# Attention layer 0: where the weighted values and projected keys are put in PSUM, and the order of TensorE, VectorE and ScalarE in a block

## The reference, cut to what matters

```
x = x + attention0(layernorm(x), ctx)      # 32 query heads of 128, 8 key/value heads
x = x + ffn0(layernorm(x))                 # fp8-like grid, 1792 inner
x = x + attention1(layernorm(x), ctx)
x = x + ffn1(layernorm(x))

attention0: q = x @ wq; k = ctx @ wk; v = ctx @ wv     # q: 32 heads, k, v: 8
            p = softmax(q k^T / sqrt(128))             # per sequence of 64
            out = concat(p v) @ wo
```

## Time and profile before

| | us |
|---|---|
| median of 3 runs | 1713.1 (1711.9 to 1725.19) |
| profiled execution | 1715.58 |
| its span | 1713.9 |
| busy PE / DVE / ACT / POOL | 1489.9 / 1325.1 / 876.0 / 477.8 |

### The profile page before, as it was taken

The page is one execution under the profiler, slowest core; times in us unless marked ns, Lnnn a source line. Parts: engine busy times, 40 slices in busy tenths (PEclk is TensorE's granted clock), DMA queues, the critical chain, the costliest instruction groups (busy, mean ns, idle before and its releaser), DMA issues. The chain is left out here.

```text
span 1713.9 us, 33213 instructions
## 1 busy us (share of the span) xinstructions
PE 1489.9 (87%) x12523; PEld 923.0 (54%) x12523; DVE 1325.1 (77%) x2414; ACT 876.0 (51%) x1825; POOL 477.8 (28%) x397
## 2 busy tenths in 40 slices
PE   5689989899899899899899986779999998677686
PEld 4456566566566666666566663334445454344343
DVE  6567767777678678668578688689999985999777
ACT  4334425335335334334335333488989863888652
POOL 4513303204214114124123101001111103689620
PEclk8799999999999999999999998989999999999898
DMA  8343435345345353453543431222222260766402
GB/s 319 141 118 119 122 106 138 104 118 136 94 121 132 94 161 93 106 172 68 143 135 84 132 142 25 100 44 44 44 56 51 43 126 1 133 103 113 86 1 98
DMA packets 283642, 178.54 MB, mean 104 GB/s; under 512 B 240240, under 2 KB 256752, under 8 KB 278768
## 3 DMA queue, kind: packets, MB, share of 16 engines
q1 hardware_dynamic: 244608, 143.49, 34.0%
q10 hardware_dynamic: 38896, 33.03, 6.2%
HBM read 102.04 MB, written 18.87 MB: 71 GB/s over the span
## 5 line engine op out<-in xcount | busy, mean ns | idle before, releaser
L806 PE MATMUL xp<-WO,OT 128*128 128x512 f16 x1536 | 345.0, 385 | 6.9 <-DVE X L1060 6.9
L700 POOL TENSOR_TENSOR QT<-QA,QT 128x512 f16<-128x512 f32 x96 | 113.5, 1196 | 646.3 <-ACT QT L884 646.3
L806 PEld LDWEIGHTS xp<-WO,OT 128*128 128x128 f16 x1536 | 149.2, 99 | 194.3 <-issue 18.7
L749 PE MATMUL xp<-XR,WQ 128*128 128x256 f16 x1536 | 185.1, 274 | 3.9 <-DVE QA L990 3.9
L909 ACT ACTIVATE E<-E 128x512 f32<-128x512 f32 x64 | 40.3, 629 | 268.2 <-DVE E L1037 268.2
L1288 PE MATMUL db<-W0T,XD 128*128 128x448 f16 x768 | 152.1, 359 | 23.1 <-DVE XD L1487 23.1
L749 PEld LDWEIGHTS xp<-XR,WQ 128*128 128x128 f16 x1536 | 148.2, 98 | 28.0 <-issue 6.1
L749 PE MATMUL pj<-XR,WQ 128*128 128x256 f16 x1152 | 143.6, 281 | 16.0 <-PEq L421 9.7
L1060 DVE SCALAR_TENSOR_TENSOR X<-xp,X 128x512 f32<-128x512 f32 x128 | 88.1, 689 | 86.2 <-PE xp L806 86.2
L1303 PE MATMUL eb<-W1T,DT 128*128 128x512 f16 x672 | 149.3, 382 | 4.2 <-ACT eb L1382 2.7
L884 ACT ACTIVATE QT<-QA 128x512 f16<-128x512 f32 x96 | 59.7, 630 | 156.0 <-DVE QA L990 156.0
(11 more groups left out here) (254 smaller groups left out, 2889.3 us busy)
## 6 DMA issues: line engine op xcount, KB each, us to landing
XR<-xsets SPq DMA_DIRECT2D x31, 1280.0 KB, 5.6
XR<-xsets SPq DMA_DIRECT2D x31, 512.0 KB, 4.5
W0T<-in_L_xattn_wq ACTq DMA_DIRECT2D x7, 1024.0 KB, 5.2
W0T<-in_L_xattn_wo ACTq DMA_DIRECT2D x7, 1024.0 KB, 6.8
CS<-in_ctx SPq DMA_DIRECT2D x4, 1024.0 KB, 10.1
X<-in_x SPq DMA_DIRECT2D x4, 1024.0 KB, 11.2
out<-X SPq DMA_DIRECT2D x8, 512.0 KB, 3.6
xsets<-XB SPq DMA_DIRECT2D x2, 1792.0 KB, 5.6
```

The lines of the kernel that those rows point to most:

```text
L700: pool.tensor_tensor(queries(1, i, j), query_sum(buffer), queries(0, i, j), ALU.subtract).then_inc(S["q_lo"], 1)
L749: last = pe.matmul(head_columns(Q_BANKS[n], m), WQ[:, a, Q_WEIGHTS[n], c, m * P:(m + 1) * P], XR[:, n, b, c, :].rearrange("p (b t) -> p b ...
L806: last = pe.matmul(xp[i % 2][:, :], OT[:, a, j, i * P:(i + 1) * P], WO[:, b, j, :], start=n == 0, stop=n == 3 * REP - 1)
```

## The change

- PE: keys go to bank tv0, values to pj1 (they wait for `add_query` 0); the second weighting goes to sc0, sc1 and follows the first directly; query products 5 and 6 come behind both. The first weighting also waits for `low_keys` of the next block (it reads tv0).
- DVE: softmax goes ahead of `add_query` 0 and `low_query`; then `add_query` 0, 1, `low_query`, `add_query` 2, `low_keys`, in t=0 the low WO, the pieces for FFN 0, `low_weights`, `low_values`, `low_out` 0, `add_query` 3, `low_out` 1, `add_query` 4. `low_q_sums` moves from POOL to DVE (t=2, after `accumulate` 1), `low_kv` to after `accumulate` 2.
- ACT: `high_keys` ahead of `high_query` 1; both `high_out` ahead of `high_query` 2, 3. `load_weights` moves from ACT's queue to SP's, behind the transposes of PT in t=0.
- Last group, t=2: `project_out` of tiles 0, 1, then the scores of the last block, then tiles 2, 3; DVE takes `accumulate` 0, 1 ahead of the last softmax.
- Opening: in blocks 1 and 2 the moments come right after the context tiles and the scales after set 3; in the last block the weights are split between the sets.

```diff
-        def low_q_sums(pool, g):
+        def low_q_sums(dve, g):
...
-                        if n == PER - 2 and blk < BLOCKS - 1:
+                        if n == (BT + 1 if blk else PER - 2) and blk < BLOCKS - 1:
                             ln_stats_scalar(act, 0, (blk + 1,))
+                        if blk == 3 and n == BT - 1:
+                            high_q(act, 0)
+                            high_kv(act, 0)
...
-                        if n == BT + 3 and blk < BLOCKS - 1:
+                        if n == (BT - 1 if blk else BT + 3) and blk < BLOCKS - 1:
                             dve.wait_ge(x_ld[blk + 1], 16)
                             ln_moments(dve, 0, blk + 1)
-                    if blk < BLOCKS - 1:
-                        ln_scales(dve, 0, blk + 1)
-                low_q(dve, 0)
-                low_kv(dve, 0)
+                        if n == (BT + 2 if blk else PER - 1) and blk < BLOCKS - 1:
+                            ln_scales(dve, 0, blk + 1)
+                        if blk == 3 and n == BT + 2:
+                            low_q(dve, 0)
+                        if blk == 3 and n == BT + 3:
+                            low_q_sums(dve, 0)
+                        if blk == 3 and n == BT + 4:
+                            low_kv(dve, 0)
...
+        weighed = (tv, sc)
...
+                    if t == 0 and g < GROUPS - 1:
+                        load_weights(sp, g)
...
             def project_keys(g, t):
-                pe.wait_ge(S["q_add"], n_of(g, t, 5, 1))
-                    last = pe.matmul(pj[1][:, :], WKV[:, a, k, 0, :], CT[:, b, k, tokens], start=n == 0, stop=n == 3 * KC - 1)
+                    last = pe.matmul(tv[0][:, :], WKV[:, a, k, 0, :], CT[:, b, k, tokens], start=n == 0, stop=n == 3 * KC - 1)
             def project_values(g, t):
-                pe.wait_ge(S["q11_lo"], n_of(g, t, 1, 1))
+                pe.wait_ge(S["q_add"], n_of(g, t, 5, 1))
...
-            def weigh_values(g, t, pair):
+            def weigh_values(g, t, pair, keys):
                 if pair == 0:
-                    pe.wait_ge(S["kv_lo"], n_of(g, t, 2, 2))
+                    pe.wait_ge(S["kv_lo"], n_of(*keys, 2, 1) if keys else n_of(g, t, 2, 2))
                     pe.wait_ge(S["pt_done"], n_of(g, t, 32, 32))
-                else:
-                    pe.wait_ge(S["ot_lo"], n_of(g, t, 4, 2))
...
-                    weigh_values(g, t, 0)
...
+                        project_values(*nxt)
+                    weigh_values(g, t, 0, nxt if more else None)
+                    weigh_values(g, t, 1, None)
                     if more:
-                        if early:
-                            project_values(*nxt)
-                        else:
-                            query_products(*nxt, (5, 6))
-                    weigh_values(g, t, 1)
-                    if early:
-                        scores(g, SPG - 1)
-                    project_out(g, t, more)
+                        query_products(*nxt, (5, 6))
+                    if last and t == SPG - 2:
+                        project_out(g, t, more, (0, 1))
+                        pe.wait_ge(S["ot_lo"], n_of(g, t, 4, 4))
+                        scores(g, SPG - 1)
+                        project_out(g, t, more, (2, 3))
+                    else:
+                        project_out(g, t, more, range(BT))
...
             def last_block(g, t):
+                accumulate(g, t - 1, 0)
+                accumulate(g, t - 1, 1)
                 scores_less_max(g, t, 0)
...
-                    if more:
-                        add_query(*nxt, 0)
                     for jp in range(2):
                         sums(g, t, jp)
                         normalise(g, t, jp)
                     low_probs(g, t, 0)
-                    if more:
-                        low_query(*nxt)
                     low_probs(g, t, 1)
                     if more:
+                        add_query(*nxt, 0)
                         add_query(*nxt, 1)
+                        low_query(*nxt)
+                        add_query(*nxt, 2)
+                        low_keys(*nxt)
...
                     low_out(g, t, 0)
                     if more:
-                            add_query(*nxt, 3)
-                            add_query(*nxt, 4)
+                        add_query(*nxt, 3)
                     low_out(g, t, 1)
+                    if more:
+                        add_query(*nxt, 4)
...
                         if i == 1 and t == SPG - 2 and not last:
+                            low_q_sums(dve, g + 1)
+                        if i == 2 and t == SPG - 2 and not last:
                             low_kv(dve, g + 1)
```

More of the change, by code:

```diff
@@ L495, in _ @@
                         sum_q(pool, 0)
-                low_q_sums(pool, 0)
             @block.tensor
@@ L647, in head_columns, with load_weights @@
             return bank[:, :].rearrange("p (b m t) -> p m b t", m=2, b=4)[:, m, :, :]
+        def load_weights(queue, g):
+            queue.wait_ge(S["xset_st3"], 16)
+            for t in range(2):
+                queue.dma_start(WB[:, 0:8, :].rearrange("p (c t) k -> p c t k", t=2)[:, :, t, :],
+                                w0[bass.ds(g * 256 + t * P, P), :].rearrange("p (c k) -> p c k", k=P)).then_inc(S["wb_ld"], 16)
+            for c in range(2):
+                queue.dma_start(WB[:, 8 + 4 * c:12 + 4 * c, :],
+                                w1[:, bass.ds(g * 256 + c * P, P)].rearrange("(t p) k -> p t k", p=P)).then_inc(S["wb2_ld"], 16)
         @block.sync
@@ L710, in group @@
                         sum_q(pool, g + 1)
-                    if t == SPG - 2:
-                        low_q_sums(pool, g + 1)
                     for n, lo, hi in prepared(t, last):
@@ L764, in project_values @@
                         own = slice(t * BLOCK + i * P, t * BLOCK + (i + 1) * P)
-                        last = pe.matmul(pj[0][:, i * P:(i + 1) * P], CT[:, a, k, own], WKV[:, b, k, 1, :],
+                        last = pe.matmul(pj[1][:, i * P:(i + 1) * P], CT[:, a, k, own], WKV[:, b, k, 1, :],
                                          start=n == 0, stop=n == 3 * KC - 1)
@@ L792, in weigh_values, with project_out @@
                             rows = slice(h * SEQ, (h + 1) * SEQ)
-                            last = pe.matmul(tv[h][:, s * 256:(s + 1) * 256], V[rows, t % 2, a, 2 * pair + s, :],
+                            last = pe.matmul(weighed[pair][h][:, s * 256:(s + 1) * 256], V[rows, t % 2, a, 2 * pair + s, :],
                                              PT[rows, b, :, 2 * pair + s, :], start=n == 0, stop=n == 2)
                 last.then_inc(S["pv_done"], 1)
-            def project_out(g, t, more):
+            def project_out(g, t, more, tiles):
                 pe.wait_ge(S["o_lo"], g + 1)
-                for i in range(BT):
+                for i in tiles:
                     pe.wait_ge(S["ot_lo"], n_of(g, t, 4, 2 * (i // 2) + 2))
@@ L815, in group @@
                         scores(g, t)
-                    early = last and t == SPG - 2
                     if more:
@@ L896, in high_out @@
                 for h in range(2):
-                    act.activation(o_out(0, pair, h), o_bank(h), ACT.Copy).then_inc(S["ot_hi"], 1)
+                    act.activation(o_out(0, pair, h), o_bank(pair, h), ACT.Copy).then_inc(S["ot_hi"], 1)
             def group(g, last):
@@ L918, in group @@
                                 high_weights(g, *p)
-                    early = last and t == SPG - 2
                     if more:
+                        high_keys(*nxt)
                         high_query(*nxt, 1)
@@ L925, in group @@
                         stats_x(act, t - 1)
-                    if t == 0 and not last:
-                        load_weights(act, g)
                     if more:
-                        high_keys(*nxt)
-                        if early:
-                            high_query(*nxt, 2)
-                            high_query(*nxt, 3)
-                        else:
-                            high_values(*nxt)
+                        high_values(*nxt)
                     high_out(g, t, 0)
+                    high_out(g, t, 1)
                     if more:
-                        if early:
-                            high_values(*nxt)
-                        else:
-                            high_query(*nxt, 2)
-                            high_query(*nxt, 3)
-                    high_out(g, t, 1)
+                        high_query(*nxt, 2)
+                        high_query(*nxt, 3)
                     if t == 1 and not last:
@@ L970, in _ @@
             high_query(0, 0, 0)
+            high_keys(0, 0)
             high_query(0, 0, 1)
-            high_keys(0, 0)
             high_values(0, 0)
@@ L1123, in group @@
                         first_x[1](dve)
-                    if more:
-                        add_query(*nxt, 2)
                     x_ahead(1)
@@ L1129, in group @@
                     if more:
```

(9 more changed lines are left out.)

30 lines of the change are left out of this document (7 added, 23 removed).

## The result

| | median, us | range | ratio to before, 95% |
|---|---|---|---|
| before | 1714.5 | 1711.9 to 1725.2 | |
| after | 1671.2 | 1669.7 to 1672.3 | 0.9735 (0.9693 to 0.9778) |

The profiled execution took 1672.3, with a span of 1670.4 at clock 0.956. I split both traces at the starts of the scores.

A forecast was written before the change was run, and what follows sets the result against it. TensorE was taken as the bound, busy 836 of 900 us. Gains of 5 (opening), 21, 2, -1, 6 (t=0 to 3) and 9 (last group) sum to 42: 1713.1 - 42 = 1671, range 1656 to 1697.

The forecast's parts named there:

- The mechanism of t=0: Loop, t=0: second weighting no longer late by 2.22, output projection 4.2 behind the first; gain 3.0 x 7 = 21.
- W: Start of a block's first weighting; in t=0 forecast at 604.6, the end of the values, against 605.24.
- e_lo: End of DVE's low_probs 1 in the softmax; forecast 0.95 sooner in t=0, with PT 4.1 behind it.
- t=1: 4.8 for 2: Loop, t=1: add_query 3, behind low_out 0 on DVE, becomes the projection's new wait; gain 0.3 x 7 = 2.
- t=2: 1.7 for -1: Loop, t=2: as t=1, but high_weights ahead of high probs 1 on ACT; projection at 669.2 against 669.07, loss 1.
- t=3: 11.0 for 6: Loop, t=3: wait for QA stays in part, first weighting at 694.3 against 695.17; gain 0.8 to 0.9, 6 over 7 blocks.
- P: Start of a block's output projection; without waits forecast 4.2 behind the start of the first weighting.
- Last group: 7.7 for 9: Last group's four blocks: 6.8 from the chain after t=2, with 1.9 of t=1 on top; 9 for the group.
- Opening: 2.6 for 5.3: Opening: sooner moments and scales, low_kv without its stall, first query products near 66.4; gain 5.3, bounds 2 and 6.
- C: Rival, chance 0.05: low_keys holds the first weighting in all 31 blocks with a next one; at 2 us, 1733.
- B: Rival, chance 0.15: add_query 3 decides the projection's start in t=0 and 3 too; loop gives 20 less, 1698.
- D: Rival, chance 0.13: low WO in t=0 and low_weights in t=3 collide with POOL's low query; 10 less gain, 1681.

The follow-up runs named there:

- loads_alone: The kernel before with only load_weights moved from ACT's queue to SP's, behind the transposes of PT in t=0; 1701.1, ratio 0.9901.
- loads_on_act: The changed kernel with load_weights back on ACT, behind high_keys and ahead of high_values; 1674.7, ratio 0.9738.
- softmax_undone: The changed kernel with add_query 0 back ahead of the sums and low_query between the two low_probs on DVE; 1659.5, ratio 0.9660.
- sums_on_pool: The changed kernel with low_q_sums back on POOL in the loop's t=2, the opening as changed; 1676.9, ratio 0.9751.
- rec_late: The changed kernel with weights_times_rec of t=2 moved on ACT behind both high_out; 1662.9, ratio 0.9697.

## Why the prediction was right, point by point

**The mechanism of t=0 held, and its size was 17.3 for 21.** The projection starts 4.05 behind the first weighting, with 4.2 forecast, and between the two the seven blocks gained 18.4 us, more than the 2.34 a block that was forecast. loads_alone shows that ACT's issue was the cause, loads_on_act that new banks and order are a second cure for it. What fell short is W. It was to come 0.64 sooner a block, with no wait for PT, and comes 3.3 us later in the sum of the seven, 7.8 us short. About half of that is more idle time inside the scores (2.9) and slower matmuls behind it (1.2), which vary from run to run. The other half is "PT arrived 4.1 after e_lo": it is 5.0 to 5.6, and PE still waits 4.5 us for PT in the seven blocks, where I had nothing. A PT later than 4.1 was named as a sign that the forecast is wrong; it cost 0.3 to 0.9 a block, inside the bound of 1 us. (The 0.3 to spare on add_query 3 is 0.5 by the prediction's own times; nothing hangs on it.) It is not the loads' place: 4.9 to 5.8 in the blocks that wait for PT with them on ACT, 4.9 to 5.5 behind XR; with softmax_undone it is 4.0 to 4.3. So all that the softmax order brought e_lo forward in t=0 was lost on the way to PT: in blocks whose first matmuls ran at full clock, e_lo is at 11.4 behind the scores instead of 12.7 to 13.0, and W at 17.0 instead of 16.8 to 17.1.

The DMA view shows where it is lost. The same six microseconds around the transposes of PT, in a t=0 of the change (454 to 460 us, e_lo at 454.12; each digit is the busy share of 0.15 us in tenths) and in a t=3 (542.3 to 548.3, e_lo at 542.44):

```profile
DMA  0000799999600999990000000000009999763348
q8 instruction: 1, 0.02, 1.8%
PT<-EH SPq DMA_TRANSPOSE x2, 3.8
```
```profile
DMA  0000599999800499999900000000059994509965
PT<-EH SPq DMA_TRANSPOSE x2, 2.8
```

The two transposes take a median of 3.8 us from issue to landing instead of 2.8. In t=0 a transfer of another queue (q8: one packet of 0.02 MB), named "instruction", falls into them. It starts 1.7 to 2.5 behind e_lo in all seven t=0 of the change, during the second transpose, and 0.7 to 1.0 behind it in before; the transposes' packets beside it take up to 2.1 us in the change, up to 1.2 in before, and 0.02 in any t=3, where no such transfer falls beside them. It comes at about the same place in the block while e_lo moves, so an earlier e_lo meets it in another transpose. No run moved it by itself: that it is the cause is likely and not shown.

**The softmax ahead of the query sums was mis-sized most.** I took e_lo 0.95 sooner in t=0 and 1, 0.55 in t=2 and 3. Against softmax_undone, which differs in this alone, e_lo is 0.0 sooner in t=2, 0.1 later in t=3, 1.2 to 1.5 sooner in t=0, where PT takes as much longer, and 1.16 in t=1, where nothing uses it. I had subtracted an operation's 0.68 from a chain in which DVE already waited for ACT. The two traces above show it to cost 7.0 us in the blocks of t=2; the medians differ by 12. In t=0 the median difference says little, as the clock there varies (below).

**t=1: 4.8 for 2.** add_query 3 ends at 610.53, 0.1 before the projection could start; I had put it 0.05 later than PE's own time. The forecast wait did not come, and the second weighting, 0.65 behind the first, gave the rest.

**t=2: 1.7 for -1, by luck.** Typical blocks went from 28.85 to 29.25, a loss of 0.4 where 0.1 was forecast, with the wait of 0.84 for add_query 3 that I had named. The sum is positive since one block of before took 33.4. There POOL's low_q_sums met another of DVE's pieces:

```profile
301.51 4.56 DVE L105 TENSOR_SCALAR VW<-VW 128x1024 uint32<-128x1024 uint32 x1
```

The accumulation behind L105 came late, the projection waited 2.41 for it, and the t=3 behind that block took 29.0 in place of 30.3 to 31.6.

**t=3: 11.0 for 6, of which 6.3 came where it was forecast, but by another path.** Summed over the seven blocks P stands 6.3 us nearer to the scores, as forecast. But I had 0.3 a block from the move of low_q_sums and 0.55 from the softmax order; it was 0.99 and nothing. L107 alone takes 0.68, not the 1.1 that I worked out from L1119. So the stall was 3.28 of its 3.96, and 1.0 of it remains when the 2.28 of low_q_sums are taken off: DVE's first reduce comes that much sooner, and e_lo with it. The right 6 is luck in its parts. Of the rest 4.1 is not the change's work on this block: idle time at the loop's turn that lay ahead of the turn's first score in before (4.4) and lies behind it now (0.3), where t=0 has it (14.1 before, 16.9 after). The wait for QA at the start is gone, not partly kept, and the new wait of 0.6 for low_kv did not come: no row of after has either. sums_on_pool and rec_late bring a wait for low_kv back (1.1 and 0.5), so it was near. In exchange the values wait 1.03 for add_query 0, which now stands behind the softmax on DVE: the later query sum has a second reader, project_values, that I had not priced. It cost nearly nothing only because PT lands at the time when the values end (W 14.76 behind the scores, 14.66 in softmax_undone).

**Last group: 7.7 for 9.** t=3 gave 6.6 for 6.8, t=1 2.2 for 1.9, t=0 0.4 for 0.3. In t=2, where I had booked nothing, P waited 4.82 and the block lost 1.4.

**Opening: 2.6 for 5.3.** The weights' part came as forecast: low_kv fell by 3.0 and low_q_sums moved without a stall. The sets' part did not: XN of block 3 started at 49.03 as said (49.1), but the splits behind it ran slower than the 11.2 a block, and scales that took 1.3 took 2.5 where they met POOL (L172 0.54 for 0.16, L174 1.13 for 0.17). The set that ACT's weight splits hold up came free at 58.1 and not 56.1, DVE's last split ended at 68.0 and not 65.8, and PE followed 1.1 later, not 0.6. The low bound of 2 was the better value.

The total of 43 (45.2 up to the end of attention 0) for 42 is thus right through errors that cancel: too much for t=0 and the opening (6.4), too little for t=1, 2 and 3 (10.5), 1.3 too much for the last group. Of the rivals, C did not occur (no weighting waits for KT), B's full wait neither; D's collision did in t=0 (3.27 for 2.28), and it was hidden. The Trainium skill, "SBUF — State Buffer", section "Who interferes with whom", says that a VectorE instruction with two SBUF inputs contends with a GpSimd one that reads SBUF. The low WO and L1038 are of that kind, and these rows agree: 3.27 for 2.28, and 1.44 for 0.69.

## What to carry to other kernels

Before moving an operation out of a chain, look whether the engine waits for another one inside that chain: if so, the operation was free there and will be late where it goes. Undo each part of a combined change by itself: of these four parts one cost time (7 us in t=2, 12 by the medians), and two removed the same wait. A queue has slots with slack and slots without: a load behind one that waits for a buffer inherits its wait.

## What the hardware showed that I had not expected

**The clock behind the loop's turn differs from turn to turn.** No run here shows what decides it. The same idle time, 2.56 and 2.54, comes before two t=0 blocks of the change; the first 24 query matmuls behind it then take 4.45 or 2.78:

```profile
326.68 1.24 PE L780 MATMUL sc<-KT,QT 128*128 128x64 f16 x37 [2.56 <-issue]
327.76 4.45 PE L754 MATMUL pj<-XR,WQ 128*128 128x256 f16 x24
...
445.76 1.24 PE L780 MATMUL sc<-KT,QT 128*128 128x64 f16 x37 [2.54 <-issue]
446.83 2.78 PE L754 MATMUL pj<-XR,WQ 128*128 128x256 f16 x24
```

The granted clock of the five microseconds behind (the eighth number) is 0.66 and 1.00, a part at the 1.2 GHz level and all at 2.4:

```profile
328.00:333.00 5.00, 5.00 (x33) 3.78 (x31) 4.83 (x9) 2.38 (x4) 0.00 (x0) 0.66 0.00 0
...
447.00:452.00 5.00, 5.00 (x48) 4.48 (x47) 4.79 (x10) 2.42 (x4) 0.00 (x0) 1.00 0.01 3
```

Summed over a run, these 24 matmuls exceed 2.78 by 4.5 in before, 5.6 in the change, and from 3.3 to 10.1 in the experiments; the idle time at the turn is 18.5, 17.2 and 15.6 to 21.6. Differences in t=0 below some 5 us are therefore not read as effects, and the distance from W to P is used instead.

**DVE's operations stretch beside POOL's.** The same 1024-column L107 took 3.96 beside POOL's low_q_sums and 0.68 without it; the same low WO 2.28 or 3.27; the same normalising 0.69, 0.85 or 1.45.
